# Attention 2 of a one-layer ViT tower: from masked full-height keys to heads in 32-row quadrants, four heads a step

## What is computed

```python
probs = softmax(xf @ Wg.T + bg)                 # 8 experts, the best two make combine
h = einsum('td,erd->ter', xf, A) + ba           # rank 16
delta = (einsum('ter,eor->to', h * combine, Bm) + combine @ bb) * (32 / 16)
qkv = xf @ Wqkv.T + bqkv + delta                # (t, 3 * 12 * 16)
attn = softmax(einsum('bhsd,bhtd->bhst', q, k) * 16 ** -0.5)
out = einsum('bhst,bhtd->bhsd', attn, v) @ Wproj.T + bproj
```

## Time and profile before

| | us |
|---|---|
| median of three runs | 4334.95 (4316.67 to 4337.84) |
| the profiled execution, its own time | 4333.73 |
| its span on the core | 4331.8 |
| PE busy | 3840.3 (89%) |
| PEld busy | 3175.7 (73%) |
| DVE busy | 2706.7 (62%) |
| ACT busy | 2232.1 (52%) |
| POOL busy | 524.0 (12%) |

### The profile page before, as it was taken

The page is one execution under the profiler, slowest core; times in us unless marked ns, Lnnn a source line. Parts: engine busy times, 40 slices in busy tenths (PEclk is TensorE's granted clock), DMA queues, the critical chain, the costliest instruction groups (busy, mean ns, idle before and its releaser), DMA issues.

```text
span 4331.8 us, 98533 instructions
## 1 busy us (share of the span) xinstructions
PE 3840.3 (89%) x38552; PEld 3175.7 (73%) x38552; DVE 2706.7 (62%) x6866; ACT 2232.1 (52%) x3969; POOL 524.0 (12%) x858
## 2 busy tenths in 40 slices
PE   4999998889988998989999889899888898899888
PEld 3777777777777777777777777777777777777776
DVE  4666666566566666665665666666656656656654
ACT  1555555555555555545545555555555555555553
POOL 1110111111101101101111011011111111111110
PEclk7999999999999999999999999999999999999997
DMA  2000000000000000000000000000000000000000
GB/s 76 8 16 8 16 8 15 15 10 14 15 8 15 16 8 15 15 8 15 8 15 16 8 15 15 8 16 15 9 15 10 14 15 10 14 15 8 15 4 4
DMA packets 26198, 60.41 MB, mean 14 GB/s; under 512 B 3534, under 2 KB 16465, under 8 KB 25714
## 3 DMA queue, kind: packets, MB, share of 16 engines
q1 hardware_dynamic: 25806, 54.14, 4.1%
...
## 4 chain that ended last, share of the span: by engine, by line
PE 72%; DVE 17%; issue 4%; ACT 4%; POOL 1%; DMA 0%; SPq 0%; DVEq 0%; ACTq 0%; POOLq 0%
PE psum L584 13%; DVE mx L922 9%; PE psum L590 7%; PE psum L513 6%; PE psum L523 6%; PE psum L618 6%; PE psum L496 6%; PE psum L557 5%; PE psum L541 3%; PE psum L648 3%; PE psum L641 2%; PE psum L620 2%; PE psum L621 2%; ACT ka L769 2%; PE psum L571 2%
## 5 line engine op out<-in xcount | busy, mean ns | idle before, releaser
L922 DVE TENSOR_REDUCE mx<-psum 99x4 f32<-99x788 f32 x768 | 707.2, 972 | 67.3 <-PE psum L541 40.3
L732 ACT ACTIVATE ebuf<-psum 99x788 f32<-99x788 f32 x768 | 605.8, 825 | 175.7 <-PE psum L573 163.9
L513 PE MATMUL psum<-hn_s,qk_w 96*128 96x197 f16 x4608 | 435.8, 252 | 1.2 <-DVE hn_s L888 1.2
...
L696 ACT ACTIVATE qk_sq<-psum 128x788 f32<-128x788 f32 x192 | 159.1, 828 | 516.0 <-PE psum L513 516.0
L513 PEld LDWEIGHTS psum<-hn_s,qk_w 96*128 96x128 f16 x4608 | 406.2, 99 | 8.8 <-DVE hn_s L888 1.5
L618 PE MATMUL psum<-hn_s,qkv_w 96*128 96x197 f16 x2304 | 342.2, 254 | 44.2 <-ACT ss L705 43.1
L523 PE MATMUL psum<-v_w,hn_s 96*99 96x384 f16 x1536 | 333.6, 376 | 30.3 <-DVE mx L922 21.8
L943 DVE TENSOR_TENSOR qk<-psum,rinv 128x197 f32<-128x197 f32 x384 | 137.9, 359 | 342.1 <-ACT rinv L741 342.1
L590 PE MATMUL psum<-out_w,qk 128*99 128x192 f32 x1536 | 286.8, 348 | 61.5 <-issue 61.3
L584 PE MATMUL psum<-ebuf,vx 98*64 98x197 f32 (+1 forms) x3072 | 332.6, 336 | 0.0
L571 PE MATMUL psum<-qa,ka 128*99 128x197 f16 x1536 | 288.9, 252 | 46.8 <-DVE qb L934 31.3
...
## 6 DMA issues: line engine op xcount, KB each, us to landing
...
out<-h SPq DMA_DIRECT2D x128, 73.5 KB
...
out<-h SPq DMA_DIRECT2D x64, 0.8 KB
...
```

The costliest lines, as they stand in the source:

```text
L513: mm = nc.tensor.matmul(ps(p, slice(0, 128), slice(at, at + NT), m // 2), qk_w[:, w, c, f:f + 128], hn_s[s][:, v, c, 0:NT], start=(n == 0) ...
L732: nc.scalar.activation(ebuf[n % EBUFS][:].rearrange("p e a t -> p e (a t)"), psum[0:TR, b:b + 2, 0:2 * NT], ACT.Exp).then_inc(done, 1)
L922: nc.vector.tensor_reduce(mx[s][:, :, 2 * i:2 * i + 2].rearrange("p a e -> p e a"), psum[0:TR, b:b + 2, 0:2 * NT].rearrange("p e (a t) -> ...
```

## The change

- q and k of attention 2 lie in quadrants: a head's 16 rows at the start of 32 rows, four heads in the 128 rows. The weights are spread over the new places in the set-up; two heads share a quadrant in the first block, and a mask of two patterns (kmask) separates them in k. q takes two blocks of ten matmuls instead of three, and k two. qh2 and ql2 (two blocks each) and kh2 and kl2 (three) stand in for qa, qb, ka, kb, high2 and low2.
- SM2 and ST2 do four heads a step, three steps each instead of six, in four banks. Each matmul has 32 rows, four of them side by side in the four quadrants. SM2 still has 24 matmuls an image. ST2 has 96 instead of 48, since its three products and the maximum are four separate matmuls now.
- ACT's exponential of an ST2 step, and DVE's maximum of an SM2 step, are two instructions each, one for the lower two banks and one for the upper two; a new signal (read_lower) tells PE of the lower half.
- DVE makes the low part in one instruction for q and three for k; its copy in NT2 is gone, and ACT's copy covers 128 rows.
- ORDER and its banks are written anew from QK2.1 on. SM.5 and NT now come after PV2.0 and M2.0, and all of ST2 before NT.
- The set-up has 12 more small DMAs, 41 small instructions on DVE for the weights where seven large ones stood, and no broadcast into kb.

```diff
-QKV2 = 2 * G2 * 128 + D
+QKV2_RAW = 2 * G2 * 128 + D
+QKV2 = 4 * 128 + D
...
-N.2 -V2@2 -SM2.0@4 -SM2.1@2 N.3 -SM2.2@0 V.0@4 -SM2.3@2 -SM2.4@0 -SM2.5@6 V.1@4 SM.0@0 -NT2@7
+N.2 -V2@2 -SM2.0@4 -SM2.1@0 N.3 V.0@4 -SM2.2@0 V.1@6 SM.0@4 -NT2@0 SM.1@6 SM.2@2 -ST2.0@4 SM.3@0
+SM.4@2 -ST2.1@4 -PV2.0@0 -M2.0 SM.5@2 -ST2.2@4 NT@1 ST.0@2 -PV2.1@0 ST.1@4 -PV2.2@1 -LA ST.2@6
...
-WIDE = ("QK", "V", "SM", "ST", "QK2", "SM2", "ST2")
+WIDE = ("QK", "V", "SM", "ST")
+QUAD = ("SM2", "ST2")
 EBUFS = 4
 
 
 def banks(p):
 
-    return range(BANK[p], BANK[p] + (2 if p[0] in WIDE else 1))
+    return range(BANK[p], BANK[p] + (4 if p[0] in QUAD else 2 if p[0] in WIDE else 1))
+
+
+def head2(u, j):
+
+    return 2 * j + u if u < 2 else 8 + j
...
-        qa, qb = two("qa", [128, G2, NTP], F16), two("qb", [128, G2, NTP], F16)
-        ka, kb = two("ka", [128, H, NTP], F16), two("kb", [128, H, NTP], F16)
+        qh2, ql2 = sb("qh2", [128, 2, NTP], F16), sb("ql2", [128, 2, NTP], F16)
+        kh2, kl2 = sb("kh2", [128, G2, NTP], F16), sb("kl2", [128, G2, NTP], F16)
+        neg_t2 = two("neg_t2", [128, NTP], F16)
+        sel2_raw, sel2 = sb("sel2_raw", [128, G2, 1]), sb("sel2", [128, G2, TR], F16)
+        kmask = sb("kmask", [128, 2])
...
+                    freed = [(b, *now.previous(users[b], p)) for b in banks(p)]
+                    for sig, q, earlier in dict.fromkeys((*reader(q, b), earlier) for b, q, earlier in freed):
+                        wait(pe, now, sig, q, earlier)
...
-                        wait(pe, now, rd_sig["QK2"], ("QK2", s, 1))
-                        wait(pe, now, ka2_ready, ("QK2", s, 1))
-                        for e in range(2):
-                            h = 2 * i + e
-                            for t in range(2):
-                                mm = nc.tensor.matmul(ps(p, slice(0, TR), slice(NT * t, NT * t + NT), e),
-                                                      qa[s][:, h // 4, tile_cols(t)],
-                                                      ka[s][:, h, 0:NT], start=True, stop=True)
+                        wait(pe, now, high_QK2, ("QK2", s, 1))
+                        for t in range(2):
+                            for j in range(4):
+                                r = slice(32 * j, 32 * j + 32)
+                                mm = nc.tensor.matmul(ps(p, slice(0, TR), slice(NT * t, NT * t + NT), j),
+                                                      qh2[r, i // 2, tile_cols(t)], kh2[r, i, 0:NT],
+                                                      start=True, stop=True)
                     elif kind in ("NT", "NT2"):
...
-                        for e in range(2):
-                            h = 2 * i + e
-                            g = h // 4
-                            for t in range(2):
-                                o = ps(p, slice(0, TR), slice(NT * t, NT * t + NT), e)
-                                nc.tensor.matmul(o, ka[s][:, h, tile_cols(t)], qa[s][:, g, 0:NT],
-                                                 start=True, stop=False)
-                                mm = nc.tensor.matmul(o, kb[s][:, h, tile_cols(t)], qb[s][:, g, 0:NT],
-                                                      start=False, stop=True)
+                        for t in range(2):
+                            terms = ((kh2[:, i, tile_cols(t)], qh2[:, i // 2, 0:NT]),
+                                     (kh2[:, i, tile_cols(t)], ql2[:, i // 2, 0:NT]),
+                                     (kl2[:, i, tile_cols(t)], qh2[:, i // 2, 0:NT]),
+                                     (sel2[:, i, :], neg_t2[s][:, 0:NT]))
+                            for n, (left, right) in enumerate(terms):
+                                for j in range(4):
+                                    r = slice(32 * j, 32 * j + 32)
+                                    mm = nc.tensor.matmul(ps(p, slice(0, TR), slice(NT * t, NT * t + NT), j),
+                                                          left[r], right[r], start=(n == 0), stop=(n == 3))
...
-                        for m in range(G2):
-                            o = ps(p, slice(0, 128), slice(NT * (m % 2), NT * (m % 2) + NT), m // 2)
-                            f = slice(128 * (G2 * i + m), 128 * (G2 * i + m) + 128)
+                        for m in range(2):
+                            o = ps(p, slice(0, 128), slice(NT * m, NT * m + NT))
+                            f = slice(128 * (2 * i + m), 128 * (2 * i + m) + 128)
...
                     elif kind == "NT2":
                         wait(act, now, pe_sig[kind], p)
-                        nc.scalar.copy(qb[s][64:128, 0, 0:NT], psum[64:128, b, 0:NT]).then_inc(neg_copied[1], 1)
+                        nc.scalar.copy(neg_t2[s][:, 0:NT], psum[:, b, 0:NT]).then_inc(done, 1)
                     elif kind in ("ST", "ST2"):
                         wait(act, now, pe_sig[kind], p)
-                        n = e_order.index(p)
-                        wait_free(act, now, e_users[n % EBUFS], exp_used)
-                        nc.scalar.activation(ebuf[n % EBUFS][:].rearrange("p e a t -> p e (a t)"),
-                                             psum[0:TR, b:b + 2, 0:2 * NT], ACT.Exp).then_inc(done, 1)
+                        for half in range(2 if kind == "ST2" else 1):
+                            n = e_order.index((p, half)) % EBUFS
+                            wait_free(act, now, e_users[n], exp_used)
+                            nc.scalar.activation(
+                                ebuf[n][:].rearrange("p e a t -> p e (a t)"),
+                                psum[0:TR, b + 2 * half:b + 2 * half + 2, 0:2 * NT], ACT.Exp
+                            ).then_inc(rd_lo[kind][1] if kind == "ST2" and half == 0 else done, 1)
...
-                        dst, f = (qa[s], QSCALE / WS) if i == 0 else (high2, 1 / WS)
-                        if i == 1:
-                            wait_free(act, now, high2_users, reader)
-                        nc.scalar.mul(dst[:, 0:2, 0:NT],
-                                      psum[:, b, 0:2 * NT].rearrange("p (m t) -> p m t", m=2), f)
-                        nc.scalar.mul(dst[:, 2, 0:NT], psum[:, b + 1, 0:NT], f).then_inc(high_QK2[1], 1)
-                        if i == 1:
-
-                            wait(act, now, high_QK2, p)
-                            for j in range(4):
-                                a = nc.scalar.mul(ka[s][:].rearrange("p (g j) t -> p g j t", j=4)[:, :, j, :],
-                                                  high2[:], masks[:, j:j + 1])
-                            a.then_inc(ka2_ready[1], 1)
+                        if i == 0:
+                            nc.scalar.mul(qh2[:, :, 0:NT], psum[:, b, 0:2 * NT].rearrange("p (m t) -> p m t", m=2),
+                                          QSCALE / WS).then_inc(high_QK2[1], 1)
+                        else:
+
+                            for u in range(2):
+                                nc.scalar.mul(kh2[:, u, 0:NT], psum[:, b, 0:NT], kmask[:, u:u + 1])
+                            nc.scalar.mul(kh2[:, 2, 0:NT], psum[:, b, NT:2 * NT], 1 / WS).then_inc(high_QK2[1], 1)
...
-                                                    -1.0, None, ALU.mult).then_inc(ready[1], 1)
-                    elif kind == "NT2":
-                        wait(dve, now, neg_copied, p)
-                        nc.vector.tensor_copy(qb[s][64:128, 1:G2, :],
-                                              qb[s][64:128, 0:1, :].broadcast_to([64, G2 - 1, NTP])
-                                              ).then_inc(done, 1)
...
+                    elif kind == "SM2":
+                        wait(dve, now, pe_sig[kind], p)
+                        for half in range(2):
+                            at = 4 * i + 2 * half
+                            nc.vector.tensor_reduce(
+                                mx[s][:, :, at:at + 2].rearrange("p a e -> p e a"),
+                                psum[0:TR, b + 2 * half:b + 2 * half + 2, 0:2 * NT].rearrange(
+                                    "p e (a t) -> p e a t", a=2),
+                                AX.X, ALU.max).then_inc(done if half else rd_lo[kind][1], 1)
+                        if i == 2:
+                            wait(dve, now, rd_sig[kind], p)
+                            rows = neg[s][:].rearrange("p a (j k) -> p a j k", j=4)[:, :, :, 0:G2]
+                            nc.vector.tensor_scalar(rows, mx[s][:].rearrange("p a (u j) -> p a j u", j=4),
+                                                    -1.0, None, ALU.mult).then_inc(mx2_ready[1], 1)
...
-                            nc.vector.tensor_copy(qb[s][0:64, 0:G2, :], qa[s][0:64, 0:G2, :])
-                            for dst, src in ((qa[s][64:128, 0:2, 0:NT], pair[64:128]),
-                                             (qa[s][64:128, 2, 0:NT], psum[64:128, b + 1, 0:NT])):
-                                a = nc.vector.scalar_tensor_tensor(out=dst, in0=src, scalar=QSCALE / WS, in1=dst,
```

(43 more changed lines are left out.)

75 lines of the change are left out of this document (44 added, 31 removed).

## The result

The changed kernel takes **4649.9 us** (median of four runs, 4632.55 to 4675.59) against 4336.4 for the kernel before on the same chip: a ratio of 1.074, interval 1.068 to 1.080. Slower was the likelier sign of the prediction, but 4650 lies above its range of 4225 to 4530. The profiled execution took 4632.55 us.

What follows compares the result with a forecast made beforehand. PE looked like the bound, but DVE was taken to set the maxima's stretch, DVE and ACT the changed stage. From 4333.7 us: -26 order, -76 today's falls, +166 new falls, +5 set-up: 4403, rounded to 4400; range 4225 to 4530.

Steps and rivals of the forecast that it cites:

- the likelier sign of the prediction: Whole kernel: slower than before by more than 22 us at chance 0.59, against 0.28 for faster.
- PE's 7.3 us an image: QK2, SM2, ST2 and the wait for ka: time spared PE, of which only 0.4 us an image would count.
- An undisturbed ST.0: Start of ST.0 without clock falls: 26.9 us after QK2.0, against 28.1 before.
- the last maximum is queued behind M2.0: Chain to ST.0 on DVE: SM.5 waits behind M2.0, ending at 9.5 us after the negation of attention 2's maxima.
- The quads: ST2: four matmuls in quadrants take 0.085 us together, as one full-height matmul does; upper bound 0.17 us.
- the rival with quadrants two and two: ST2: quadrants run as two pairs, 88 us on top of the forecast, 4490 us; chance 0.07.
- the price of the clock: New clock falls on V.0 and at ST.0, and the loop's end: 2.6 us an image, 166 us in all.
- the prediction's 4237: Whole kernel if the clock holds, without new falls: 4237 us; as a rival, chance 0.25.
- the clock stays at half from V.0 to ST.0: V.0 to ST.0: half clock throughout, 6 us an image on 4237, 4620 us; chance 0.06.
- Chain theory: Experiments' theory: exponential pairs, M2.0, SM.5's maximum and NT set ST.0, and the clock only follows; no chance given.
- clock theory: Experiments' theory: the time went to PE's gaps ahead of V.0 and the half clock behind them; no chance given.
- Set-up: Before the loop, once: more small instructions and DMAs, no broadcast to kb, 5 us more, between 0 and 10.

Runs made afterwards that it cites:

- experiment 8: Kernel before, with SM.5 moved behind PV2.0 and M2.0 in ORDER: 4672.2 us, ratio 1.080.
- 12: Changed kernel in its own order, plus never-read matmuls, 18 ahead of SM2.1 and 5 ahead of ST2.0: 4366.4 us, ratio 1.008 to the kernel before.
- 7: Kernel before, without the low-part products of V.0 and V.1 (16 of 24 matmuls): 4310.4 us, ratio 0.996.
- 5: Changed kernel, SM.5 ahead of ST2.1, PV2.0, M2.0 and NT ahead of ST2.2, plus 18 never-read matmuls before SM2.1, 5 before ST2.0: 4073.2 us.
- 6: Changed kernel with SM.5 ahead of ST2.1, PV2.0 and M2.0, NT ahead of ST2.2, no extra matmuls: 4455.2 us, ratio 1.028 to the kernel before.
- 11: Changed kernel with V.0, V.1, SM.5 and NT moved earlier and SM2.2 ahead of SM.0, no extra matmuls: 4304.2 us, ratio 0.993 to the kernel before.
- 4: Changed kernel with V.0, V.1, SM.5 and NT moved earlier, SM.0 ahead of SM2.2, no extra matmuls: 4432.2 us, ratio 1.024 to the kernel before.

## Why the prediction was wrong in size

**What held.** PE's 7.3 us an image brought nothing, since DVE and ACT set the stage. QK2.0 to SM2.0 is 6.3 us (said: 6.4), with no wait for ACT. The first maximum of SM2 comes at 8.6 us (9.2), V.0 at 9.7 behind a maximum (10.1); the three kl2 products took 0.418, 0.418 and 0.356 us (0.38). An undisturbed ST.0 comes at 26.8 us (26.9), and DVE waits for M2.0 with SM.5's maximum behind it, as in the chain that was written down. The step "the last maximum is queued behind M2.0" is confirmed as costly by experiment 8.

**The quads.** I kept 0.085 us for four quadrants, by the rows. A quad is four matmuls side by side in the four quadrants. ST2 in the changed kernel, the first three quads and the eighth:

```profile
1918.17 0.29 PE L592 MATMUL psum<-qh,kh 32*99 32x197 f16 x4 [0.90 <-DVE mx L961]
1918.29 0.25 PE L592 MATMUL psum<-ql,kh 32*99 32x197 f16 x4
1918.38 0.25 PE L592 MATMUL psum<-qh,kl 32*99 32x197 f16 x4
...
1918.80 0.25 PE L592 MATMUL psum<-neg_t,sel 32*99 32x197 f16 x4
```

Over eight quads 1918.17 to 1918.80 is 0.63 us for seven steps: 0.12 for the first and 0.085 for each of the others, as before for single full-height matmuls. The 3.07-fold speedup that the Trainium skill gives for four row tiles ("TensorE: Matmul & The Clock Gate", section "Measured speedup vs the span model") does not show at 197 columns; the rival with quadrants two and two falls too.

**What failed** is a term of the sum, the price of the clock. I had the falls in place: one on V.0, one at ST.0, behind the gaps that I had counted. But I took their lengths from the kernel before ("a fall of 3.4 us costs 1.7 us, one of 6.6 twice that") and charged the first with 0.6 us, "where PE has 0.7 us of lead", 2.6 us an image for all. In the runs the clock, once down at V.0, stays down for 17 us or more in 49 of 63 half passes, through the chain to within a few microseconds of ST.0 or past it. The changed kernel spends 1528 / 64 = 23.9 us an image at half clock, where my two falls of 3.4 to 6.6 us make 13 at the most. The mean half pass is 4.8 us longer instead of 1.1 (the forecast's 70 us over 64 images). In the terms of the sum: undisturbed, the half pass was to take 64.7 - 0.4 = 64.3 us, and the new falls 2.6 on top; it took 70.7, so the term of 2.6 measured about 6.4. The 64.3 was not run by itself, but it fits: 12 has 515 us at half clock left, and at 0.2 to 0.3 us for each (the last section) an estimate for that order without falls is 4212 to 4263 us, around the prediction's 4237. A clock that stays low through the chain was the rival that I gave 0.06: "the clock stays at half from V.0 to ST.0", 4620 us; 4633 was the profiled time. Against it I had held that V.0 and V.1 fill PE at half clock and that the fall of the earlier trace rows ended after 6.22 busy us of 6.60. That second argument was one sample, and it failed: the fall went on with PE busy for 6.45 of 7.0 us on V.0 and V.1, and behind them comes a stretch in which PE waits for DVE and ACT, busy for 5.15 of 6.50 us even at half clock. In the kernel before, the stretch behind the gap had more of PE's work, and its falls were short; the change took 5.7 us of PE's work off QK2, SM2 and ST2. That less work there makes falls longer is borne out in part by 7. What ended a fall after 3.4 us in one half pass and after 27.3 in another of the same order stays open.

The experiments weigh it. Extra matmuls add work to PE, spare none and leave every other engine's work as it is, so what they gain is put down to the clock. They alone, with no dependency changed, take 283 us off the changed kernel (12), and 382 off the reordered one (5 against 6). The order of SM.5, M2.0 and NT is worth 195 us without them (6) and 293 with them (5 against 12). Chain theory and clock theory each hold for a part; by the estimate under 12 the chain's own part of what 5 gained is some 140 us, and the larger part is the clock's. But the miss against the forecast is the clock's: the chain had been priced, and its ST.0 came at 26.8 us as computed. The changed layout itself is no loss: with the better order and with PE kept at work it is 6% faster than before, and 4.6% faster than the kernel before with its own extra matmuls (4073 against 4271). The kernel before was not given a better order, so how much of this is the layout's is not shown.

**Set-up** was forecast at 5 us more; the first QK2.0 comes 2.4 us earlier (136.56 against 138.97). It moves by as much between runs that share the set-up (133.26 in 6, 139.68 in 11), so this bounds the term but doesn't measure it.

**Left open.** Whether real work could fill both gaps: only two orders of V and SM were tried (4, 11), none together with extra matmuls. And what decides how long a fall lasts.
